# Keys turned by VectorE like the queries, both loaded in runs of 64 numbers, one transfer per sequence

## The reference, cut to what matters

```
q    = x + braak_embed[itok][..., None]          # x: 32 x 256 x 256, a number per sequence and row
attn = softmax(einsum('bsd,btd->bst', q, side))  # side: 32 x 256 x 256, keys
o    = einsum('bst,btd->bsd', attn, side)        # and the same array as values
out  = x + moe_ffn(rmsnorm(o) ...)               # 8 experts, top 2, low-rank updates, F = 1024
```

## Time and profile before

| what | before |
|---|---|
| median of three runs | 1297.7 us (1297.67 to 1297.9) |
| the profiled execution | 1297.99 us, its span 1296.2 us |
| PE busy | 1290.6 us, 100% |
| DVE busy | 857.3 us, 66% |
| ACT busy | 531.0 us, 41% |
| POOL busy | 232.2 us, 18% |
| share of PE in the chain that ended last | 99% |
| q1 (all loads and stores of SyncE) | 116020 packets, 68.54 MB, 19.2% of 16 engines |

### The profile page before, as it was taken

The page is one execution under the profiler, slowest core; times in us unless marked ns, Lnnn a source line. Parts: engine busy times, 40 slices in busy tenths (PEclk is TensorE's granted clock), DMA queues, the critical chain, the costliest instruction groups (busy, mean ns, idle before and its releaser), DMA issues.

```text
span 1296.2 us, 18613 instructions
## 1 busy us (share of the span) xinstructions
PE 1290.6 (100%) x7190; PEld 1128.8 (87%) x7190; DVE 857.3 (66%) x1582; ACT 531.0 (41%) x991; POOL 232.2 (18%) x189
## 2 busy tenths in 40 slices
PE   9999999999999999999999999999999999999998
PEld 8999988888888888888888888888888888888887
DVE  6898756656665666656665766566665776575656
ACT  6877744324333334333433333333433333333332
POOL 3444530202020200202020202020110202020200
PEclk9999999999999999999999999999999999999999
DMA  9777730010202020102011020202020101102000
GB/s 287 160 170 170 178 97 1 30 46 1 74 2 73 1 73 2 60 15 48 26 31 45 1 74 2 73 1 74 2 62 12 54 21 39 37 3 71 1 17 17
DMA packets 116419, 69.73 MB, mean 54 GB/s; under 512 B 57694, under 2 KB 107372, under 8 KB 116204
## 3 DMA queue, kind: packets, MB, share of 16 engines
q1 hardware_dynamic: 116020, 68.54, 19.2%
q10 hardware_dynamic: 312, 0.02, 0.0%
HBM read 51.40 MB, written 17.14 MB: 53 GB/s over the span
## 4 chain that ended last, share of the span: by engine, by line
PE 99%; ACT 0%; DVE 0%; issue 0%; DVEq 0%
PE bank L1295 31%; PE bank L1294 31%; PE bank L1296 31%; PE bank L1421 2%; PE bank L1347 1%; PE bank L1399 1%; PE bank L1340 1%; PE bank L1306 0%; ACT prob L739 0%; PE bank L1386 0%; DVE x_out L1238 0%; ACT qT_hi L722 0%; PE bank L1314 0%; PE bank L1429 0%; PE bank L1428 0%; PE bank L1364 0%
## 5 line engine op out<-in xcount | busy, mean ns | idle before, releaser
L1166 DVE TENSOR_TENSOR act_a<-silu_a,bank 128x512 f32<-128x512 f32 x128 | 87.7, 685 | 211.6 <-PE bank L1296 195.0
L830 ACT ACTIVATE br_hi<-act_br 128x512 fp32r<-128x512 f32 x128 | 80.9, 632 | 188.0 <-DVE act_br L1177 188.0
L823 ACT ACTIVATE silu_b<-bank 128x512 f32<-128x512 f32 x128 | 76.2, 595 | 187.9 <-PE bank L1296 187.1
L1295 PE MATMUL bank<-w2T_lo,s_hi 128*128 128x256 f32 x512 | 144.7, 283 | 0.0
L1296 PE MATMUL bank<-w2T_hi,s_lo 128*128 128x256 f32 x512 | 143.3, 280 | 0.0
L1294 PE MATMUL bank<-w2T_hi,s_hi 128*128 128x256 f32 x512 | 142.7, 279 | 0.0
L1174 DVE TENSOR_TENSOR act_b<-silu_b,bank 128x512 f32<-128x512 f32 x128 | 88.0, 687 | 80.9 <-PE bank L1296 80.0
L660 POOL TENSOR_TENSOR t_lo<-t_in,t_hi 128x512 fp32r<-128x512 f32 x32 | 40.6, 1290 | 552.5 <-ACT t_hi L810 552.3
L819 ACT ACTIVATE silu_a<-bank 128x512 f32<-128x512 f32 x128 | 75.7, 591 | 134.8 <-PE bank L1296 134.7
L679 POOL TENSOR_TENSOR v_lo<-v_full,v_hi 128x512 fp32r<-128x512 f32 x64 | 94.6, 1510 | 136.6 <-ACT v_hi L815 136.6
L1187 DVE TENSOR_TENSOR br_lo<-act_br,br_hi 128x512 fp32r<-128x512 f32 x128 | 104.8, 819 | 5.6 <-ACT br_hi L830 3.1
(11 more groups left out here) (201 smaller groups left out, 3215.6 us busy)
## 6 DMA issues: line engine op xcount, KB each, us to landing
kv<-in_fside_BxSxS SPq DMA_DIRECT2D x32, 256.0 KB, 3.1
t_scratch<-oT SPq DMA_DIRECT2D x32, 256.0 KB, 2.5
t_in<-t_scratch SPq DMA_DIRECT2D x32, 256.0 KB
out<-x_out SPq DMA_DIRECT2D x52, 128.0 KB
x_in<-in_x SPq DMA_DIRECT2D x96, 64.0 KB, 2.7
x_out<-in_x SPq DMA_DIRECT2D x48, 128.0 KB
rho<-scale_scratch SPq DMA_DIRECT2D x16, 256.0 KB
rstd<-scale_scratch SPq DMA_DIRECT2D x16, 256.0 KB
```

The lines of the kernel that those rows point to most:

```text
L823: nc.scalar.activation(silu_b[:, :], h1_bank[j % 2][:, :], ACT.Silu).then_inc(silu_b_ready, 1)
L830: nc.scalar.activation(br_hi[j % 2][:, :], act_br[j % 2][:, :], ACT.Copy).then_inc(br_hi_ready, 1)
L1166: nc.vector.tensor_tensor(act_a[j % 2][:, :], silu_a[j % 2][:, :], h3_bank[j % 2][:, :], ALU.mult).then_inc(act_a_ready, 1)
L1295: nc.tensor.matmul(dst, w_hi, x_lo, start=False, stop=False, skip_group_check=not grouped)
```

## The change

For sequences 6 to 29:

- `load_k` is new: the keys are loaded a second time, into `k_in` (three buffers), in the interleaved order. `turn_k` is new: VectorE turns them straight into `kT_bank` in PSUM. TensorE's four key transposes are gone.
- The feature order becomes (g, c, b) instead of (c, g, b), so that a run is 64 numbers (256 B) and one transfer brings a sequence: `x_blocks` and `side_blocks`, 4 x 256 x 64 numbers each.
- Keys and values for the weighted sum are loaded by `side_mixed`, 4 x 64 x 256, to match the order of the turned keys.
- The low part of the turned query moves from VectorE (L950) to GpSimd (`turned_q_low`), between the bias and `value_low`.
- The joint semaphores of queries and keys are split; ScalarE makes the high parts of turned queries and keys without waiting for TensorE.

```diff
-            x_blocks = x.rearrange("b (s j) (c g a) -> b g s (j c) a", s=BLK, c=DC, a=BLK)
+            x_blocks = x.rearrange("b (s j) (g y) -> b g (s j) y", s=BLK, y=DC * BLK)
+            side_blocks = side.rearrange("b (s j) (g y) -> b g (s j) y", s=BLK, y=DC * BLK)
+            side_mixed = side.rearrange("b (s h j) d -> b j (s h) d", s=BLK, h=SC)
...
                 if c in TURNED:
-                    for g in range(P // BLK):
-                        sp.dma_start(x_in[c % RING][g * BLK:(g + 1) * BLK].rearrange("p h (n a) -> p (h n) a", a=BLK),
-                                     x_blocks[c, g]).then_inc(xs_loaded[c % RING], 16)
+                    sp.dma_start(as_blocks(x_in[c % RING][:, :, :]).rearrange("p (j y) -> p j y", j=BLOCKS), x_blocks[c]
+                                 ).then_inc(xs_loaded[c % RING], 16)
...
+                if c in TURNED:
+                    sp.dma_start(kv[c % RING][:, :, :], side_mixed[c]).then_inc(kv_loaded[c % RING], 16)
+                    return
...
+            def load_k(c):
+                if c - K_RING in TURNED:
+                    sp.wait_ge(k_turned, turned_no(c - K_RING))
+                sp.dma_start(k_in[c % K_RING][:, :].rearrange("p (j y) -> p j y", j=BLOCKS), side_blocks[c]
+                             ).then_inc(k_loaded[c % K_RING], 16)
...
             def step(c):
+                if c + 4 in TURNED:
+                    load_k(c + 4)
                 if 5 <= c + 3 < BATCH:
                     load_kv(c + 3)
...
+            def turned_q_low(c):
+                pool.wait_ge(qT_hi_ready, c + 1)
+                hi, lo = qT[c % 2]
+                nc.gpsimd.tensor_tensor(in_blocks(lo[:, :]), blocks_of(q[c % 2][:, :, :]), f32(in_blocks(hi[:, :])),
+                                        ALU.subtract).then_inc(qT_lo_ready, 1)
...
+            def turn_k(c):
+                dve.wait_ge(k_loaded[c % K_RING], k_count(c))
+                dve.wait_ge(kT_hi_ready, c)
+                dve.wait_ge(kT_lo_ready, c)
+                nc.vector.transpose(kT_bank[:, :], k_in[c % K_RING][:, :]).then_inc(k_turned, 1)
...
                 if c + 2 in TURNED:
                     turn_q(c + 2)
+                    turn_k(c + 2)
...
                 if c + 1 < BATCH:
-                    transpose_qk(c + 1)
+                    if c + 1 not in TURNED:
+                        transpose_q(c + 1)
+                        transpose_k(c + 1)
```

## The result

| | before | after |
|---|---|---|
| median | 1297.8 us (1297.67 to 1298.82) | 1462.9 us (1460.24 to 1464.46, four runs) |
| ratio | | 1.1268, 95% interval 1.1249 to 1.1288 |
| span of the profiled execution | 1296.2 us | 1462.7 us |
| first product of the second stage | 167.63 us | 333.46 us |

The prediction was 1468.7 us, by four DMA engines that carry every new load. The time and the mechanism are as predicted; two of the sum's terms are not, and that the errors nearly cancel is luck. The second stage lasts 1462.7 - 333.46 = 1129.2 us, before 1128.6, as predicted.

A forecast was written before the change was run, and what follows sets the result against it. Four DMA engines were to bound the attention of sequences 6 to 29: 1298.0 + 167.0 (later turn of 29) + 4 (slower clock) = 1469.0 us, 1468.7 against the median; range 1415 to 1550.

The forecast's parts named there:

- Four engines: Loads of sequences 6 to 29: every new load runs on the same four DMA engines, 11.9 us per sequence against TensorE's 4.20.
- The fourth rival: New loads: each takes four engines, but different ones; 1291.7 us; chance 0.10 together with the sixteen-engine rival.
- 256 B packet: Loads of x and turned keys: a 256 B run takes 16.5 ns on an engine, 4.22 us per load.
- The second and third rival: Packet time in x and key loads: 256 B costs as 512 B, 1559 us, 0.12; or as 128 B, 1425 us, 0.08.
- Values: Load of keys and values per turned sequence: 64 x 41.5 ns, 2.66 us on each of four engines.
- SyncE doesn't leave them idle: Transfer queue of the first stage: SyncE has two more batches queued when it waits, so the four engines always have work.
- Hidden gain: Key transposes off TensorE in 24 sequences: 10.3 us saved, but hidden behind the transfers and not in the sum.
- Sixteen engines, 1291.7: First rival, new loads: they run on sixteen engines, 3.6 us per sequence, TensorE's 4.20 stands; chance 0.10 with different groups of four.
- The 4 us for what VectorE holds back: Routing steps, sixteen-engine rival: VectorE operations wait for GpSimd's new subtraction, 0 to 8 us, taken as 4.
- The tail: From the turn of sequence 29 to the second stage: 19.6 us, plus 0 to 15 for a slower clock, taken as 4.
- Loads that take under 3 us: After the turn of sequence 29: two plain sequences' loads take under 3 us, so that stretch is mostly unchanged.
- TensorE busy a third: From about 35 to 315 us: TensorE is busy a third of that stretch, a sign of the four-engine bound.

The follow-up runs named there:

- the split runs: Changed kernel, loads cut into four transfers on sixteen engines: all loads 1396.0 us; x and keys only 1357.4; values only 1453.3.
- the run with split values: Changed kernel with only the load of keys and values cut into four transfers on sixteen engines: 1453.3 us, ratio 1.1186.
- the runs with plain rows: Changed kernel, new loads as whole 1 KB rows on sixteen engines: 1296.0 us; also with the query's low part back on VectorE: 1295.1 us.
- four keys: Kernel before with only the keys of sequences 8, 9, 10 and 22 turned by VectorE, loads on sixteen engines: 1299.7 us, ratio 1.0017.

## Why the prediction was right, and where it wasn't

**Four engines: shown.** The count of reports, two engines at half the rate, and sixteen in the split runs all follow from the outermost dimension. By the Trainium skill, "DMA: Bandwidth & Descriptors", section "Why a DMA increments its semaphore by 16 and not by 1", the largest divisor up to 16 counts; the runs agree, with 72 GB/s for 4 and 36 for 2. The fourth rival, different groups for different transfers, is out: with two halves of a load issued one behind the other, the rate is still 36 GB/s.

**256 B packet: mis-sized.** The line between 128 and 512 B gave 16.5 ns, measured 14.1. x and keys take 3.6 us each instead of 4.22. The two ends of that line were got in two ways: 23.8 ns is a count on engines that always had work, 12.9 ns is a share, and a share counts the overlap of packets too. Taken from the share, 256 B are 0.32 x 16 x 2.2 / 623 = 18.1 ns here, and 512 B are 1.12 x 16 x 0.7 / 471 = 26.6; the line between 12.9 and 26.6 gives 17.5 for 256 B, near what is measured. That points to a sound line whose lower end was too high for a count. What a packet of 128 B costs an engine by count no run shows. The second and third rival were the ends of this term.

**Values: mis-sized the other way.** The step of 11.71 us, less twice 3.6 and the store's 0.79, leaves 3.7 us for the values' load instead of 2.66. Its packets are seen in a window of 0.7 us, 204.4 to 205.1:

```profile
DMA packets 66, 0.07 MB, mean 97 GB/s; under 512 B 0, under 2 KB 66, under 8 KB 66
```

0.7 x 4 / 66 = 42 ns, the 41.5 of the sum. In the two windows of the same length ahead of it there are 38 and 41 packets: the load starts at little more than half its rate. At 41.5 ns these 79 packets are 0.8 of 1.4 us, so about 0.6 us are lost there. The rest of the missing 1 us isn't the values': after the store the rate of the small packets is lower too, 62 GB/s from 210.5 to 211.7 us. Why either is so isn't shown. Both errors together are 0.2 us per step, 5 us in the sum: the turn of 29 was predicted for 315.1 and is at 309.68.

**"SyncE doesn't leave them idle": wrong as said.** Two batches are not queued; SyncE is held in its instructions. In the changed kernel the four engines had work nearly all the time nevertheless: 7.2 + 2.66 + 0.79 = 10.65 of 11.71 us. In the run with split values the same thing cost 62 us against expectation. The step lacked a row: no transfer of the kernel before waits to be issued for long.

**Hidden gain: right.** The 10.3 us are not in the time, and the runs with plain rows show that they weren't whole either.

**Sixteen engines, 1291.7: the rival's premise was incomplete.** One transfer on sixteen engines isn't to be had with these views, and split loads meet SyncE: six transfers of 0.64 us are 3.84 of 4.63 us in the kernel before already, ten took 5.95 in the step shown. The 4 us for what VectorE holds back were too small: with plain rows 8 of the 10.3 us are lost, the end of its range. How much of that is the lock isn't separated. The lock alone doesn't decide: with the low part on VectorE 7 to 8 us are lost as well, since VectorE is full.

**The tail: the size right, the reason half.** From the turn of 29 to the second stage 333.46 - 309.68 = 23.8 us, before 19.55: 4.2 more, 4 predicted, all for the slow clock. The clock is there: granted 0.51 from 309.66 to 315.00, near the 1.2 GHz level, after a wait of 6.95 us. The scores of sequence 28 and the gate products at that clock, and the scores of 29 at the full one:

```profile
310.93 0.58 PE L1356 MATMUL bank<-kT_hi,qT_hi 128*128 128x256 f32 x1 [6.95 <-POOL qT_lo L657]
...
313.65 1.68 PE L1480 MATMUL bank<-oT 128*128 128x136 f32 x8
315.08 0.37 PE L1356 MATMUL bank<-probT_hi,value_hi 128*128 128x256 f32 x1
...
319.12 0.38 PE L1356 MATMUL bank<-kT_hi,qT_hi 128*128 128x256 f32 x1 [1.93 <-POOL qT_lo L657]
...
320.63 0.60 PE L1409 MATMUL bank<-ident,q 128*128 128x128 f32 x4
```

From start to start twelve scores take 2.72 us for 1.51, the gate 1.43 for the 0.84 of the kernel before: the clock costs 1.8 us, not 4. TensorE then stood 1.93 us for the low part of sequence 29, which GpSimd makes behind the bias of sequence 30, whose x came late:

```profile
316.00 1.83 POOL L671 TENSOR_SCALAR q<-x_in,bias 128x256 f32<-128x256 f32 x2 [3.89 <-DMA x_in<-in_x]
```

"Loads that take under 3 us" overlooked that they are queued behind the others. Another 0.8 us is that the scores of 28 begin 1.25 us after the turn of 29, before 0.47, as they wait for a low part too. One set of key transposes, 0.49 us, is gone in between, and that leaves 0.2 us unexplained. That 4 came out is luck.

**"TensorE busy a third": wrong.** It is 56.09 of 100 us, at a mean granted clock of 0.76: part of the work runs at the lower level, where a product takes 0.41 us for 0.28. It cost nothing there, as it lay in the wait.

## What to carry to other kernels

Before merging small transfers into a large one, read how many engines the new view will use: its outermost dimension decides, and the reports in the packet row tell it for a view that is already there. Count SyncE's transfers per step as a budget of its own (0.6 us each here): this kernel had 0.8 us left in a step of 4.63. That another engine issues some of them wasn't tried. Take a packet's time from a count in a stretch where the engines always have work, and don't mix it with one taken from the share. And a saving on the fullest engine can be given back in a later stretch that something else paces, as with four keys here.

## What the runs showed of the hardware that was not expected

- A packet of 256 B takes 14.1 ns on an engine, on two engines as on four, by count.
- SyncE is held in the issue of a transfer when large transfers on four engines are outstanding, 6.25 us in the step shown and up to 6.8 in the changed kernel; in the steps of the split runs shown it takes 0.45 to 0.65 us for each.
- Turning 128x512 numbers from SBUF to PSUM takes 0.684 us on VectorE, to SBUF 0.712: the write to PSUM costs nothing, as the sum had it (0.70).
- The packet intervals of one engine overlap: four engines with packets of 256 B show a share of 0.32, not 0.25. A share alone, times 16, would have said five engines, and a packet time of 18.1 ns for 14.1.
